# The squared sum of an FFN's hidden tile folded once more on VectorE, and the first layer's weight split moved to an earlier place in GpSimd's order

## What is computed

```python
x = x + 0.5 * ffn(layernorm(x), w_up, w_down)        # first FFN stage
x = x + attention_layers(layernorm(x))               # eight layers, each with its own weights
x = x + 0.5 * ffn(layernorm(x), w_up, w_down)        # last FFN stage

def ffn(x, w_up, w_down):
    h = gelu(ternary_linear(x, w_up))                # 128 -> 512
    return ternary_linear(h, w_down)                 # 512 -> 128

def ternary_linear(x, w):                            # w_q: entries -1, 0 or 1
    rms = sqrt(sum(x * x, axis=-1)) / sqrt(d)
    return (x / (rms + 1e-8)) @ w_q.T
```

## Time and profile before

| | us |
|---|---|
| median of three runs | 934.0 (932.17 to 934.82) |
| profiled execution, its own time | 936.12 |
| span of the profiled execution, first to last instruction | 934.3 |
| TensorE matmul busy | 865.6 (93%) |
| VectorE busy | 813.2 (87%) |
| ScalarE busy | 795.5 (85%) |
| GpSimd busy | 441.9 (47%) |

### The profile page before, as it was taken

One profiled execution on the slowest core, in us unless ns is written; L12 is line 12 of the kernel. 1 busy time (PEld: TensorE's weight loads), 2 busy tenths in 40 slices (PEclk: granted clock), 3 DMA queues, 4 the chain that ended last, 5 costly groups with the idle time before them and its releaser, 6 DMA issues.

```text
span 934.3 us, 14522 instructions
## 1 busy us (share of the span) xinstructions
PE 865.6 (93%) x4043; PEld 613.2 (66%) x4043; DVE 813.2 (87%) x3333; ACT 795.5 (85%) x1138; POOL 441.9 (47%) x561
## 2 busy tenths in 40 slices
PE   3999358999999999999999999999999999995898
PEld 2899235666666666666666666666666666653797
DVE  6477456999999999999999999999999999967553
ACT  3685477999999999999999999999999999742873
POOL 3242702455555555455555555555555445433221
PEclk8799678999999999999999999999999999995999
DMA  5000100000000000000000000000000000000011
GB/s 151 1 1 1 33 1 1 9 1 15 20 1 15 1 21 1 14 13 9 1 15 12 9 4 12 20 1 15 1 12 1 1 1 0 1 1 0 13 34 46
DMA packets 19518, 12.05 MB, mean 13 GB/s; under 512 B 1160, under 2 KB 18288, under 8 KB 19440
## 3 DMA queue, kind: packets, MB, share of 16 engines
q1 hardware_dynamic: 19440, 11.13, 4.1%
HBM read 9.03 MB, written 2.10 MB: 12 GB/s over the span
## 4 chain that ended last, share of the span: by engine, by line
DVE 64%; PE 19%; issue 7%; ACT 6%; POOL 2%; DMA 0%; SPq 0%; DVEq 0%; ACTq 0%; POOLq 0%
DVE z L859 16%; DVE st L845 10%; PE bank L542 6%; DVE phi_k L982 5%; DVE x_fm L1069 5%; DVE kvf L993 4%; DVE phi_q L972 4%; DVE mv L852 4%; DVE e L965 4%; DVE vf L1034 3%; PE bank L556 3%; DVE x_hi L1077 3%; PE bank L392 3%; DVE y L1042 2%; PE bank L529 2%
## 5 line engine op out<-in xcount | busy, mean ns | idle before, releaser
L1300 POOL TENSOR_TENSOR x_lo<-x_fm,x_hi 128x512 fp32r<-128x512 f32 x120 | 155.5, 1305 | 261.0 <-DVE x_hi L1077 261.0
L493 PE MATMUL bank<-h,w 128*128 128x512 f32 x512 | 260.5, 593 | 0.0
L737 ACT ACTIVATE h<-bank,par 128x512 f32<-128x512 f32 x256 | 167.1, 693 | 11.7 <-PE bank L400 10.6
L859 DVE TENSOR_SCALAR z<-bank,mv,rstd 128x128 f32<-128x128 f32 x512 | 169.4, 403 | 8.4 <-POOL rstd L1292 8.2
L398 PE MATMUL bank<-x_hi,w_hi 128*128 128x512 f32 x256 | 151.6, 592 | 1.6 <-ACT h L737 1.6
L1292 POOL TENSOR_TENSOR rstd<-ve,minus_half 128x4 f32<-128x4 f32 x128 | 132.7, 1037 | 10.7
L398 PE MATMUL bank<-x_hi,wqkv_hi 128*128 128x512 f32 x192 | 107.6, 560 | 17.0 <-DVE phi_q L972 10.0
L845 DVE BATCH_NORM_STATS2 st<-bank 128x6 f32<-128x128 f32 x512 | 113.3, 285 | 1.0 <-PE bank L392 0.9
L392 PEld LDWEIGHTS bank<-ident,y 128*128 128x128 f32 x512 | 62.4, 141 | 59.9 <-ACT x_fm L753 23.4
L400 PE MATMUL bank<-x_hi,w_lo 128*128 128x512 f32 x256 | 101.1, 395 | 0.0
L399 PE MATMUL bank<-x_lo,w_hi 128*128 128x512 f32 x256 | 100.9, 394 | 0.0
(11 more groups left out here) (101 smaller groups left out, 1797.3 us busy)
## 6 DMA issues: line engine op xcount, KB each, us to landing
x_tm<-in_x SPq DMA_DIRECT2D x8, 256.0 KB, 3.8
raw_w<-in_W SPq DMA_DIRECT2D x8, 256.0 KB, 2.7
w<-in_W SPq DMA_DIRECT2D x8, 256.0 KB, 2.8
out<-x_tm SPq DMA_DIRECT2D x8, 256.0 KB, 2.3
raw_qkv<-in_Wk SPq DMA_DIRECT2D x8, 64.0 KB, 1.8
raw_qkv<-in_Wq SPq DMA_DIRECT2D x8, 64.0 KB, 2.0
raw_qkv<-in_Wv SPq DMA_DIRECT2D x8, 64.0 KB, 1.9
wo<-in_Wo SPq DMA_DIRECT2D x8, 64.0 KB, 2.5
```

Source lines behind the costliest of these rows:

```text
L493: mm = pe.matmul(m.ps_o[:, :], m.w2[T.weights][:, c, :], m.h[:, T.par, c, :], start=c == 0, stop=c == FC - 1)
L737: act.activation(m.h[:, T.par, c, :], m.ps_h[c % 2][:, :], ACT.Gelu_apprx_tanh, bias=column(m, B1, T.layer, c, FC)).then_inc(s.gelu_h[T.pa ...
L859: last = dve.tensor_scalar(dst[:, j, :], src(j), mv[:, j, 0:1], scale[:, j:j + 1], ALU.subtract, ALU.mult)
L1300: pool.tensor_tensor(m.x_lo[:, T.slot, :], m.x_fm[:, T.slot, :], m.x_hi[:, T.slot, :].bitcast(F32), ALU.subtract).then_inc(done, 1)
```

## The change

In the FFN, VectorE adds twice: 1,024 columns as before (into hss, which now has one buffer instead of two), then, after a wait on that add's semaphore, the two chunks of hss to one of 512 columns (hsum, two buffers). TensorE waits for the second add and makes four one-column products per tile instead of eight, each from one 128-column block of hsum, with no accumulation. A new wait on the tile before's second add stands ahead of the first one. The two constants that place layer 0's weight split change from -19 and -1 to -29 and -29: the six pairs now stand in GpSimd's list between ticks -30 and -29.

```diff
--- before.py
+++ after.py
@@ -14,7 +14,7 @@
 JOBS = LAYERS * NT
 TICKS = JOBS // 2
 TICKS_IN = NT // 2
-TICK_QKV, TICK_W1 = -19, -1
+TICK_QKV, TICK_W1 = -29, -29
 FIRST_TICK, END_TICK = -34, 58
 KEY, QUERY, VALUE = 0, 1, 2
 EXP_AND_LN = "natural_log_exp_and_others"
@@ -279,7 +279,8 @@
         m.zc = [sb(f"zc_{x}", [2, TILE], F32R) for x in ("hi", "lo")]
         m.fh = sb("fh", [2, FC, TILE])
         m.hsq = sb("hsq", [FC, TILE])
-        m.hss = sb("hss", [2, 2, TILE])
+        m.hss = sb("hss", [2, TILE])
+        m.hsum = sb("hsum", [2, TILE])
         m.scale = sb("scale", [2, 8, BLK])
         m.fz = sb("fz", [2, BLK, P])
         m.fst = sb("fst", [2, BLK, 6])
@@ -323,6 +324,7 @@
     f.gelu = [sem(f"ffn_{tag}_gelu{i}") for i in range(2)]
     f.hsq = sem(f"ffn_{tag}_hsq")
     f.hss = sem(f"ffn_{tag}_hss")
+    f.hsum = sem(f"ffn_{tag}_hsum")
     f.ssq = sem(f"ffn_{tag}_ssq")
     f.down = sem(f"ffn_{tag}_down")
     f.ms = sem(f"ffn_{tag}_ms")
@@ -550,11 +552,9 @@
             return
         emptied(pe, left, "q")
         left["q"] = (F.f.ms, F.n)
-        pe.wait_ge(F.f.hss, F.n)
+        pe.wait_ge(F.f.hsum, F.n)
         for j in range(BLK):
-            for i in range(2):
-                last = pe.matmul(m.ps_q[:, j:j + 1], m.hss[:, F.par, i, j * P:(j + 1) * P], m.ones[:, 0:1],
-                                 start=i == 0, stop=i == 1)
+            last = pe.matmul(m.ps_q[:, j:j + 1], m.hsum[:, F.par, j * P:(j + 1) * P], m.ones[:, 0:1], start=True, stop=True)
         last.then_inc(F.f.ssq, 1)
 
     def turn_c(F):
@@ -1088,8 +1088,11 @@
         if not F:
             return
         at_least(dve, F.f.ssq, F.n - 2)
+        at_least(dve, F.f.hsum, F.n - 1)
         dve.wait_ge(F.f.hsq, F.n)
-        dve.tensor_tensor(m.hss[:, F.par, :, :], m.hsq[:, 0:2, :], m.hsq[:, 2:4, :], ALU.add).then_inc(F.f.hss, 1)
+        dve.tensor_tensor(m.hss[:, :, :], m.hsq[:, 0:2, :], m.hsq[:, 2:4, :], ALU.add).then_inc(F.f.hss, 1)
+        dve.wait_ge(F.f.hss, F.n)
+        dve.tensor_tensor(m.hsum[:, F.par, :], m.hss[:, 0, :], m.hss[:, 1, :], ALU.add).then_inc(F.f.hsum, 1)
 
     def mean_square(F):
         if not F:
```

## The result

The changed kernel takes 926.34 us (median of four runs, 925.39 to 928.71) beside 933.09 us for the kernel before in the same rounds: a ratio of 0.993, interval 0.9908 to 0.9952. Timed again later, in other rounds, it took 928.76 us (927.95 to 929.58, five runs) beside 934.84: 0.9939, interval 0.9927 to 0.9951. It is faster by 5.7 to 6.5 us of 934.0; the forecast was 8.3. The profiled execution of the first launch took 928.71 us.

What follows compares the result with a forecast made beforehand. TensorE was taken to bound the first and last FFN stages, GpSimd's weight split the hand-over to layer 0. Gains of 5.9 + 1.4 + 1.0 = 8.3 us against the median 934.0 gave 925.7 us, range 919.5 to 930.8.

Steps and rivals of the forecast that it cites:

- Part 1: Hand-over to layer 0: weight split moved into GpSimd's idle stretch, so the first projection needn't wait for it; gain 5.9 us.
- part 2: Squares in both FFN stages: second add on VectorE, four products instead of eight on TensorE; gains 1.4 and 1.0 us.
- The third rival: Hand-over gives only the three QKV pairs' 2.35 us, something else holding the first projection: 929.3 us; chance 0.06.
- Part 2, last stage: Last FFN stage: shorter squares win 1.6 us over the pairs, a later residual returns 0.6; gain 1.0 us.
- Part 2, first stage: First FFN stage: gain at its beginning, five later tiles give 0.5 us back; gain 1.4 us.
- Tiles 0 and 1: Beginning of the first stage, where TensorE's queue alone counts: tile 0 gives 1.05 us, tile 1 gives 0.85.
- Tile 4 to tile 5 (and 2 to 3) is set by ScalarE: First stage: ScalarE's gelus wait for a down product ahead of tile 2's squares, so shortening those moves nothing.
- The replay of tile 3 to tile 4: First stage, one period stepped through: VectorE's queue delays squares and z_lo; add to add grows from 7.33 to 7.4 us.
- The clock: Sign of being wrong: granted clock below 1.00 from 36 to 81 us through TensorE's pauses, costing more than all else.
- The fourth rival: First stage: split steps hold up tile 5's two adds by up to 0.45 us each: 926.6 us; chance 0.06.
- The first two rivals: Both FFN stages: all TensorE's shortening arrives, 914.1 us, chance 0.08; or VectorE's queue fully binds, 939.9 us, chance 0.04.

Runs made afterwards that it cites:

- the split alone: The kernel before with only layer 0's weight split moved to tick -29, squares unchanged: 927.85 us, 0.9926 of the kernel before.
- the squares alone: The changed kernel with the weight split put back at ticks -19 and -1, second add kept: 933.15 us, 0.9983 of the kernel before.
- both adds moved: The changed kernel with both adds of the last stage's odd tiles placed behind the mean square and z_lo in VectorE's list: 923.87 us, 0.9887.
- the busy wait: The changed kernel with eight unread 512-column products on TensorE between the last tile's squares and its down products: 927.41 us, 0.9922.
- two tiles of the first stage: The changed kernel with the last stage's odd-tile adds behind z_lo and, in the first stage, the second add only for tiles 0 and 1: 922.05 us, 0.9867.
- W1 left: The changed kernel with only the three QKV pairs at tick -29, the W1 pairs staying in tick -1: 927.61 us, 0.9921.

## Why the prediction was right, and where its sizes were off

The forecast was 925.7 us in a range of 919.5 to 930.8, faster at 0.92; both medians lie in the range and its sign holds. Part 1 carries it. That 925.7 lies so near 926.34 is in part chance: of a gain of 8.3 us 5.7 to 6.5 came, part 2 gave nothing on top of the split in the times, and the kernel before ran 0.9 us faster in those rounds than the 934.0 that the forecast started from.

**Part 1, 5.9 us (4.5 to 6.5).** Met. The hand-over shrank by 6.27 us by the rows, and the split alone is 6.9 us faster (interval 5.5 to 8.2). The cover was where it was said to be: six pairs in 4.7 us plus the stretched rows, from 65.05 to 71.05, and the rms of tile 5 waits for VectorE at 72.71. The 0.4 us above 5.9 is the start of the projection inside the turn's 1.09 us, which the prediction had as its upper end. One small cost was not in the sum: in the five profiled executions with the split moved and the eight products on tiles 2 to 7, the add of tile 7 comes 7.47 to 7.50 us behind that of tile 6, in the kernel before 7.12. The third rival (only 2.35 us) is out.

**Part 2, last stage, 1.0 us (-0.8 to 3).** Met up to the last down products, for the reasons given. From the first squares to the last down products the split alone takes 917.34 - 865.17 = 52.17 us, the changed kernel 916.02 - 864.80 = 51.22: 0.95. Per pair it is 0.54 (0.5 forecast); the wait for z_lo is there; the last products come 5.89 us behind the squares of tile 6 instead of 5.28, 0.61 late as forecast. What the sum did not have is the length of these products: they were taken at full clock, 3.82 us, and took 6.66 in both profiled executions of the changed kernel, 2.84 more, so that the stage as a whole loses 1.9 us there, beyond the end of -0.8. The split alone and the squares alone show 3.82 and 3.84. The forecast wrote of the clock only for the first stage.

**Part 2, first stage, 1.4 us (-0.5 to 3.5).** This step failed: no gain shows. In the times, the second add on all tiles and on none stand at 923.87 and 924.01 us with the same last stage. In the rows, from the first add to the turn, the changed kernel takes 75.14 us and the split alone 74.47, 0.67 less, but the former alone had a stretch at the clock of 0.83. Over the profiled executions it is 74.9 to 75.8 with the second add on all tiles and 74.5 to 77.3 with none. Three terms of the step:
- Tiles 0 and 1 were priced at 1.05 + 0.85 = 1.9 us. Rows show 0.92 for the two up to the add of tile 2 (with all tiles 1.24), and where runs of like clock are compared this is tile 1's. Tile 0's shortening reached tile 1 and was gone at tile 2; the last section has the rows.
- "Tile 4 to tile 5 (and 2 to 3) is set by ScalarE ... shortening them moves nothing" holds as far as it goes: the add of an odd tile starts 8.15 to 8.19 us behind the down product that ScalarE's gelu waits for, with the second add and without it (59.23 to 67.42 in the changed kernel, 59.64 to 67.80 in the split alone). What the step did not ask is what the second add does to that down product. It comes behind the up product that waits 0.43 us for z_lo (58.20), and z_lo stands on VectorE behind the second add; the period from tile 4 to tile 5 grew from 7.94 to 8.33 us. The replay of tile 3 to tile 4 met each wait it named (7.32 us against 7.4 forecast; squares 0.31, up product 0.43), but a period has two halves, and only one had been replayed. The 8.45 us from tile 2 to tile 3 are no such cost: where tile 2 came later they were 7.95 with the second add on all tiles, too (43.76 to 51.71, both adds moved). The size came out near the forecast: tiles 2 to 7 cost 0.34 to 0.64 us at full clock, where 0.5 was given back.
- The clock: "a granted clock below 1.00 between 36 and 81 us, because TensorE now pauses" was named as what would prove the text wrong, and the sum of this part had nothing for it. It came: in the changed kernel squares(5) waits 1.17 us at 69.74 and the down products at 71.64 take 3.23 us, where other halves take 1.95. The period from tile 5 to tile 6 is 9.31 us, against 8.37 with full clock. "More than all of this" was too much: it is 0.9 us there and 1.1 to 2.0 in the stage. That the pause brings it is not shown: behind the same wait (1.17 us at 69.67 with both adds moved, 1.18 at 69.72 with the busy wait) the down products took 1.95, and half of the executions without the second add on tiles 2 to 7 had such a stretch later on.

**The fourth rival.** The split steps were to hold up the adds of tile 5 by 0.9 us. They did by 0.09 + 0.14 = 0.23; it is GpSimd that waited, 0.85 + 0.46 us, in time it had to spare. The run without W1 pairs there has both adds at their usual length, which shows the cause. The Trainium skill (SBUF — State Buffer, Who interferes with whom) has the second instruction to issue blocked until the first has ended. The rows bear that out in part: w_lo, which issued 0.31 us into the first add, ended 0.30 us after the add's end at 68.74, where a whole step takes 0.46; the adds were held for less than a whole step.

**The first two rivals** are out as they stood, but the first shows what is there: with both adds of the odd tile behind z_lo, TensorE's shortening arrives in the last stage in full, 13.84 us a pair against 15.65, and the whole kernel takes 922.05 us with two tiles of the first stage. That version has the lowest median of those run, 0.9867 of the kernel before (its interval overlaps those of the other three with this order and the second add in the last stage), and is faster than the changed kernel's 928.76 in the same rounds. The stage from its first squares to its last down products takes 47.1 us there, 4.1 less than in the changed kernel.

## What to carry to other kernels

Work taken from a full engine and given to one with slack arrives only if the receiver's in-order queue has that slack at that place: look at what stands behind the added instruction and who waits for it, in every phase of the period (here even and odd tiles), and if need be put the added work behind those entries, as the last stage shows (0.95 us won in the given order, 5.1 in the better one: 52.17 to 47.1). Where the receiver's queue is the bound, the work may as well stay where it was (here 1.8 us less by medians, with intervals that overlap). Preparation that fits into an idle stretch belongs ahead of the wait that ends it: the split alone won as much as the whole change.

## What the runs showed that was not expected

- The granted clock (full 2.4 GHz, half 1.2 GHz) falls in some executions and not in others of much the same work. Ahead of the last down products TensorE waited 1.61 us in four profiled executions: the products took 6.66 and 6.65 us in two and 3.84 in two. With 1.32 and with 0.27 us they took 5.47; with 0.60, in four, 3.84; with no wait 3.82 (kernel before, split alone) and 3.73. Between the changed kernel and the run with W1 left, whose last stages have the same instructions, that is 2.8 us, as much as a measurement can tell. What decides it stays open.
- The same in layer 0: the mean clock from 112 to 160 us lies between 0.76 and 0.89 over the thirteen profiled executions, the kernel before at the lowest (with the split moved, the same work lies some 5 to 10 us earlier in that window). Its profiled execution stands 2.1 us above its median, and part of the gain seen between the two profiles is that.
- A tile's shortening at the very start did not last: with the second add on tile 0 alone, the add of tile 1 came 8.89 us behind that of tile 0 instead of 10.18, and that of tile 2 at 18.15, as without it. The clock had been 0.76 from 26 to 31 us and 0.55 from 31 to 36 there, 0.50 and 0.68 in the split alone.
